# A semaphore in place of GpSimd's drains, and the weights of the sums in two small VectorE instructions

## What is computed

```
g = groupnorm(x)                 # 32 groups of 8 channels, over channels and pixels of the group
s = 0.5*(|g[.,w+1]-g[.,w-1]| + |g[h+1,.]-g[h-1,.]|) + 0.5*|g|     # zero padding
sp = mean of s over each patch of 32 x 32 pixels                   # 8 x 8 patches
mask = the 128 of 256 channels with the largest sp, for each patch
out = x + g * mask
```

## Time and profile before

| | us |
|---|---|
| median of 3 runs | 2892.66 (2890.99 to 2894.01) |
| the profiled execution, its own time | 2896.18 |
| span in its trace | 2894.4 |
| first ten tiles, to the L660 of tile 10 | 273.8 |
| the 53 tiles from there to the L660 of tile 63 | 2445.9 (46.1 each) |
| from there to the end: last tile and ten blocks | 174.7 |
| DMA busy share, mean clock granted to PE | 65%, 0.79 |

### The profile page before, as it was taken

One profiled execution on the slowest core, in us unless ns is written; L12 is line 12 of the kernel. 1 busy time (PEld: TensorE's weight loads), 2 busy tenths in 40 slices (PEclk: granted clock), 3 DMA queues, 4 the chain that ended last, 5 costly groups with the idle time before them and its releaser, 6 DMA issues.

```text
span 2894.4 us, 18679 instructions
## 1 busy us (share of the span) xinstructions
PE 1700.1 (59%) x4304; PEld 829.2 (29%) x4304; DVE 1717.7 (59%) x3318; ACT 1601.7 (55%) x2561; POOL 1450.1 (50%) x1635
## 2 busy tenths in 40 slices
PE   6998576534655556755355555676647746567800
PEld 3444232212222223322122222333323322233300
DVE  8999586435554557755345464676636655568710
ACT  5776367534544446756345454556746645446953
POOL 7565265234454535634245353555435544446666
PEclk9999788766877788877687777788878868788955
DMA  9999856774746474566774646546765546465685
GB/s 396 397 407 405 368 198 265 307 312 192 289 181 273 176 278 189 215 255 265 308 297 193 262 193 249 213 174 253 282 269 210 218 181 273 169 253 193 243 326 192
DMA packets 95872, 746.74 MB, mean 258 GB/s; under 512 B 25256, under 2 KB 25256, under 8 KB 76176
## 3 DMA queue, kind: packets, MB, share of 16 engines
q1 hardware_dynamic: 22032, 536.88, 46.4%
q0 software_dynamic: 73728, 208.66, 18.6%
HBM read 427.82 MB, written 402.65 MB: 287 GB/s over the span
## 4 chain that ended last, share of the span: by engine, by line
issue 47%; POOL 20%; DVE 19%; POOLq 6%; DMA 4%; PE 2%; DVEq 1%; ACT 1%; another core or an unknown queue 0%; SPq 0%; ACTq 0%
DVE larger L669 9%; POOL slots L350 9%; POOL out_dram L365 6%; DVE stats L649 5%; POOLq L384 2%; POOL ends L328 2%; DMA ring<-in_x_dram 2%; DVEq L637 1%; DVE sums L676 1%; DVE sums L686 1%; DVE record L652 1%; POOL rstd L383 1%; DMA slots<-in_x_dram,rows 1%; POOL place L320 1%; PE vertical L512 1%
## 5 line engine op out<-in xcount | busy, mean ns | idle before, releaser
L512 PE MATMUL vertical<-ring,plus 128*128 128x512 f32 (+2 forms) x1536 | 860.8, 645 | 0.0
L513 PE MATMUL vertical<-ring,minus 128*128 128x512 f32 (+2 forms) x1536 | 813.8, 614 | 0.0
L599 ACT ACTIVATE place<-place 128x960 f32<-128x960 f32 x192 | 190.6, 993 | 1032.0 <-POOL place L320 1032.0
L669 DVE SCALAR_TENSOR_TENSOR larger<-ring 128x960 bf16<-128x960 f32 x448 | 627.1, 1441 | 16.3 <-issue 0.5
L649 DVE BATCH_NORM_STATS2 stats<-ring 128x6 f32<-128x512 f32 x1024 | 630.0, 677 | 10.1 <-DMA ring<-in_x_dram 9.9
L615 ACT ACTIVATE thrown<-ring,record 128x1024 bf16<-128x1024 f32 x512 | 581.6, 1136 | 1.6
L676 DVE TENSOR_REDUCE sums<-ends 128x7 f32<-128x448 f32 x64 | 39.5, 616 | 909.1 <-POOL ends L328 909.1
L475 PE MATMUL rank_bank<-record,averager 128*128 128x1 f32 x128 | 33.9, 334 | 886.4 <-DVE record L652 886.4
L385 POOL TENSOR_TENSOR newton<-rstd 128x1 f32<-128x1 f32 x64 | 12.3, 193 | 963.9 <-issue 962.5
L320 POOL TENSOR_TENSOR place<-ring 128x960 f32<-128x960 f32 x192 | 486.6, 2534 | 0.7 <-ACT place L599 0.7
L609 ACT ACTIVATE vertical<-vertical 128x960 f32<-128x960 f32 x384 | 365.1, 951 | 165.7 <-PE vertical L513 165.4
(11 more groups left out here) (97 smaller groups left out, 1334.7 us busy)
## 6 DMA issues: line engine op xcount, KB each, us to landing
ring<-in_x_dram SPq DMA_DIRECT2D x63, 4096.0 KB, 15.7
out_dram<-ring SPq DMA_DIRECT2D x42, 4096.0 KB, 26.1
out_dram<-ring SPq DMA_DIRECT2D x32, 2048.0 KB, 6.6
out_dram<-in_x_dram SPq DMA_DIRECT2D x12, 2048.0 KB, 56.4
ring<-in_x_dram SPq DMA_DIRECT2D x4, 1024.0 KB, 7.7
slots<-in_x_dram,rows POOLq DMA_INDIRECT x256, 17.0
out_dram<-slots,rows POOLq DMA_INDIRECT x256, 12.0
```

The costliest lines, as they stand in the source:

```text
L512: nc.tensor.matmul(to, plus[:], a, start=True, stop=False)
L513: done = nc.tensor.matmul(to, minus[:], b, start=False, stop=True)
L599: nc.scalar.activation(v, v, ACT.Abs, accum_out=sums[r][:, DOWN, w:w + 1])\
L669: nc.vector.scalar_tensor_tensor(out=larger[w % 3][:].rearrange("p (r c) -> p r c", r=PATCH), in0=xs[:, w, :, 2:], scalar=0.0, in1=xs[:, w ...
```

## The change

GpSimd's seven drains a tile go. Each operation in front of one now increments a new semaphore, `scale_step`, and GpSimd waits for its count before it goes on. On DVE the weighing of all eight kinds at once (L699, two inputs of 128 x 64) goes, and `total` adds `sums` directly, with one drain less. Instead `weigh` multiplies two kinds in place by a constant, 128 x 7 numbers each: MEANS before `minus_mean`, LARGER at the end of the step behind one more drain. The constants that held the weights go, and with them four small memsets at the start.

```diff
-WEIGHTS = {LARGER: 2.0, MEANS: -2.0 * (BN // 2)}
...
+            scale_steps = [0]
+
+            def then(ins):
+
+                scale_steps[0] += 1
+                ins.then_inc(scale_step, 1)
+                pool.wait_ge(scale_step, scale_steps[0])
+
...
-                nc.gpsimd.tensor_tensor(away[:], part_mean, nm, ALU.add)
-                pool.drain()
-                nc.gpsimd.tensor_tensor(newton[:], away[:], away[:], ALU.mult)
-                pool.drain()
+                then(nc.gpsimd.tensor_tensor(away[:], part_mean, nm, ALU.add))
+                then(nc.gpsimd.tensor_tensor(newton[:], away[:], away[:], ALU.mult))
...
-                nc.gpsimd.tensor_tensor(rstd[:], var[:], minus_half[:], ALU.pow)
-                pool.drain()
-                nc.gpsimd.tensor_tensor(newton[:], rstd[:], rstd[:], ALU.mult)
-                pool.drain()
...
+                then(nc.gpsimd.tensor_tensor(rstd[:], var[:], minus_half[:], ALU.pow))
+                then(nc.gpsimd.tensor_tensor(newton[:], rstd[:], rstd[:], ALU.mult))
+                then(nc.gpsimd.tensor_tensor(correction[:], newton[:], var[:], ALU.mult))
+                then(nc.gpsimd.tensor_scalar(newton[:], correction[:], -0.5, 1.5, ALU.mult, ALU.add))
+                then(nc.gpsimd.tensor_tensor(now, rstd[:], newton[:], ALU.mult))
...
+            def weigh(tile, kind, weight):
+
+                these = sums[tile % RING][:, kind, 0:ACROSS]
+                nc.vector.tensor_scalar(these, these, weight, None, ALU.mult)
+
...
-                nc.vector.tensor_tensor(weighed[:], sums[tile % RING],
-                                        weights[:].unsqueeze(2).broadcast_to([PARTS, KINDS, COLS]), ALU.mult)\
+                nc.vector.tensor_reduce(totals[:], sums[tile % RING].rearrange("p k w -> p w k"), AX.X, ALU.add)\
                     .then_inc(recorded, 1)
-                settle()
-                nc.vector.tensor_reduce(totals[:], weighed[:].rearrange("p k w -> p w k"), AX.X, ALU.add)
...
+                    if tile + 1 < ALL_TILES:
+                        weigh(tile + 1, MEANS, -2.0 * (BN // 2))
                     minus_mean(tile + 1)
                     columns_at_edge(tile)
+                    settle()
+                    weigh(tile, LARGER, 2.0)
```

More of the change, by code:

```diff
@@ L148, in groupnorm_patch_topk @@
         minus_half = sb("minus_half", [PARTS, 1])
-        weights = sb("weights", [PARTS, KINDS])
         place_numbers = sb("place_numbers", [PATCHES, 1], INT32)
@@ L157, in groupnorm_patch_topk @@
         sums = [all_sums[:, b] for b in range(RING)]
-        weighed = sb("weighed", [PARTS, KINDS, COLS])
         totals = sb("totals", [PARTS, COLS])
@@ L219, in groupnorm_patch_topk @@
         scale_ready = sem("scale_ready")
+        scale_step = sem("scale_step")
         by_band_ready = sem("by_band_ready")
@@ L232, in groupnorm_patch_topk @@
         block = ctx.enter_context(nc.Block())
-        CONSTANTS = 26 + len(WEIGHTS)
+        CONSTANTS = 25
         x_rows = x.rearrange("t p (w f) -> (t p w) f", w=COLS)
@@ L284, in _ @@
             make(nc.gpsimd.memset(factors[:], 0.0))
-            make(nc.gpsimd.memset(weights[:], 1.0))
-            for kind, weight in WEIGHTS.items():
-                make(nc.gpsimd.memset(weights[:, kind:kind + 1], weight))
             make(nc.gpsimd.memset(same_channel[:], 1.0))
@@ L823, in _ @@
             statistics(0, 3)
+            settle()
+            weigh(0, MEANS, -2.0 * (BN // 2))
             minus_mean(0)
```

## The result

The changed kernel takes 2292.81 us in the median of four runs (2290.89 to 2296.80), against 2892.01 before: a ratio of 0.7929, 95% interval 0.7915 to 0.7943. The forecast was 2329 with 2060 to 2600 around it. The profiled execution has a span of 2289.6 us.

The account below looks back on a forecast made before the run. It took GpSimd's drain behind the pow, waiting for outstanding gathers and scatters, as the bound. Gains by stretches of tiles sum to -564 us from 2896.2, so 2332, less 3.5 for the median: 2329 us, range 2060 to 2600.

Parts of the forecast that it names:

- What holds the kernel before: GpSimd's drain behind the pow waits for all outstanding gathers and scatters, 962.5 us; ACT and DVE wait for GpSimd.
- Part 1(a): Semaphore replacing the drain behind GpSimd's pow comes when the pow ends; bounds 0 to the whole 962.5 us gained.
- Part 1(b): GpSimd's other six drains a tile turned into semaphores: 0, bounds -40 to +75 us.
- Part 2: DVE's weighing L699 replaced by two small multiplies: 0, bounds -134 us to +2 us for each multiply.
- rival E: The two-port rule lets GpSimd hold both new DVE multiplies in each tile: 2450 us, 2%.
- What is late next: Gathers missing a bulk burst land 24 us into the next; cycles of 48 and 26 us, 36 a full tile.
- rival A: Gathers land in time and DMA alone is the limit: 2050 us, 10%.
- Rival B: Every gather of a full tile misses, 48 us for all 22 such tiles: 2590 us, 8%.
- Rivals C and D: C: GpSimd's semaphore is held like the drain, 2893 us, 3%; D: scatters are starved too, 3490 us, 2%.
- The stages: Gains by stretches of tiles, from the starts of L660, summing to -564 us.
- What would show it: Signs in the new profile, such as uneven tile steps near 26 and 48 us and DMA at some 80%.
- The wait on ACT: Sign: ACT's L570 waits for gathers tens of times, 20 us and more each, several hundred us in all.

Follow-up runs that it names:

- the combined version: Changed kernel with each bulk load and store cut into four, ACT's scale-and-offset operations last in a tile, GpSimd's transfers behind the scale's chain: 2055.5 us.
- eighths: Changed kernel with each bulk load and store issued as eight transfers of 4 KB a partition instead of one of 32 KB: 2080.0 us.

## Why the prediction was right, and where it was not

**What holds the kernel before.** Shown. The wait is one for what GpSimd's queue still has outstanding. With a semaphore in place of the first drain the wait moved to the next one, one drain restored it, and with none it is gone. In all 54 waits of the kernel before, the operation behind the drain starts 0.3 to 0.8 us after the last gather has landed. The prediction says "gathers and scatters": in each of the 54 every scatter had landed 4 us or more earlier, so that a scatter alone would hold a drain is not shown. Two small misreadings of the page change nothing in the sum: GpSimd is busy 50% and not 55 to 60, and the third largest wait is PE's weight load (911.9 us), just ahead of DVE's.

**Part 1(a), the semaphore is not held.** Right: the pow's took effect 0.08 us after it (731.15 less 730.49 + 0.58). But that the wait belongs to the drain behind the pow was true only by its place. The prediction said that the other drains stand where nothing is outstanding; the four behind the second to fifth operations stand there as well, and cost little only because the first had waited already. For the change as made it is the same, as it replaces them all.

**Part 1(b), six other steps at 0.** A step of the chain is 0.27 us from start to start with a semaphore, 0.34 with a drain. The -0.07 is in the bounds, but 384 such steps make 27 us where nothing hides them, so 0 was too small a size for this term. The kernel with one drain back, which keeps 25 us with the sums' 2.5 in them, agrees.

**Part 2, the sums at 0.** This term was mis-sized: 2.5 us with the drains, some 30 without, inside the bounds of -134. The reason for 0 (DVE waits for GpSimd at L676 anyway) was read from a trace in which it waited 909 us there; that wait is 42.3 now. By the rule on the shared port pair in the Trainium skill, "SBUF — State Buffer", section "SBUF: two separate sides", GpSimd could also hold the new instructions. The trace agrees, in rare cases. The new line's duration (ns, min/median/max):

```profile
L695 DVE TENSOR_SCALAR sums<-sums x128: 150/170/3850, 16.4 to 2150.7; 128x7 f32<-128x7 f32 x128
```

Five of the 128 lasted over 1 us, one of them 3.85, and each ended 0.03 us before an operation of GpSimd did; but the sum over all 128 is 30.1 us, so rival E is out for this kernel. It depends on what GpSimd does at that moment: with its transfers moved behind the scale, 25 of the 128 lasted over 1 us, 89.4 us in all.

**What is late next.** Right in kind and nearly in size. The gathers that miss a burst of the bulk queue were the step that decides between 2050 and 2329. Two different edits, one of which gives the gather more time and one of which only changes the bulk's packets, each removed the alternation of 28 and 45 us. The forecast had 48 and 26 us, mean 36; measured 45.9 and 28.2, and 36.0 in the mean of tiles 19 to 26, of which three are long. Inside the long tile two errors cancel: the gather landed 28.8 us into the burst, not 24, and ACT got through 14.6 us of work before the next tile began, not 24. The rest of ACT's work fell into the next tile, so that ACT sets this one too (busy 28.2 of 28.2 us) where the forecast had the loop or DMA. The pair is 74.1 us against 74. DMA alone as the limit (rival A, 2050) is excluded for this kernel; it is about what the best version reaches. Rival B is out, the long tiles alternate. Rivals C and D are out, the latter by 10.9 us of waiting for scatters in all.

**The stages.** Predicted and measured: to tile 13, 380 and 377.5; tiles 13 to 16, 136 and 136.8; 17 and 18, 109 and 99.4; 19 to 26, 288 and 287.7; tiles 49 to 52, 122 and 119.3. Three more were off: tiles 53 to 58 took 197.7 us for 216, as only one of the six was long; tiles 33 and 34, the like of 17 and 18, took 95.2 for 109.5; tiles 27 and 28 took 62.8 for 57. Tiles 17 and 18, 33 and 34, and 53 to 58 make 42 us too much, and smaller errors go both ways, which is why the forecast is 36 us from the measured time. The kernel with the semaphores alone is the one for which part 2 is rightly 0, and it took 2324.3 us against the forecast's 2329. But its stages are off as well, 10 us less than forecast for tiles 17 and 18 and 10 more for 27 and 28, and cancel. With errors of 6 to 18 us in single stages, the closeness of the total is partly luck.

**What would show it.** The median from issue to landing was to rise from 17.0 to 20 us or more. The changed kernel's trace has no landing times for the gathers, so this sign can't be read there. In the kernel with semaphores alone, whose tiles go the same way, the median is 16.8, though the longest rose from 47.6 to 69.6: most gathers are on time, and a median does not show the late ones. The wait on ACT was the better sign: 27 waits, 469 us.

**Left open.** What holds eighths and the combined version at 2055 to 2080 us was not tried. DMA is busy 91 to 92% of their spans, and DVE 90% from 400 to 1900 us in the combined one (1348 of 1500); no run tells the two apart. DVE's busy time is not all work: an instruction of L665, for one, takes 1.15 us at its lowest and 1.67 in the mean in the changed kernel.

## What to carry to other kernels

A drain on GpSimd waited here for every gather still under way, so behind gathers order small operations by a semaphore; and replace all of the drains there, as the first that is left takes over the whole wait. When a long wait goes, work out in which order the transfers that it used to hide are served: a queue with small rows beside one with large rows got a turn for each packet here, not a share of the bytes. Cutting the large ones was worth 9% of the changed kernel's time, giving the small ones more time 3%, and 7% with GpSimd's transfers moved as well; both together 10%. An edit that is worth next to nothing under a long wait should be judged again once the wait is gone.

## What the runs showed that I had not expected

The wait of a drain ends with the landing of the last gather issued ahead of it, and what is waited does not grow with the number of drains: seven 962.5 us, one 1005.3. It need not cost anything in the end: ahead of the gathers 299.0 us of it left the time unchanged. The two DMA queues moved the same number of packets, within 1%, in the stretches shown for all four sizes (395:394, 744:741, 457:460, 742:748); the Trainium skill, "DMA: Bandwidth & Descriptors", section "Queues, rings and completion order", states turns by packet but takes a packet to be several descriptors. Here the counts fit turns of one packet of the profile, which is one row of one partition, 32 KB or 4 KB, or a packet under 512 bytes. And bulk packets of 16 and 8 KB cost nothing that could be seen (1319, 1321 and 1325 us of the 16 engines), while those of 4 KB took 4% more of DMA's time (1378 us).
